# Expert stage of a four-block network: the residual rows of X enter PSUM by identity products, and the output's transposes add onto them

## The reference, cut to what matters

```python
def _L0_ffn_ref(x, Wr, Wg, Wu, Wd, Sg, Su, Sd, expert_bias):
    ...
    rw = jnp.zeros_like(logits).at[jnp.arange(T)[:, None], top_i].set(probs)   # two of eight experts
    gate = jnp.einsum('td,edf->tef', xf, Wg)
    up = jnp.einsum('td,edf->tef', xf, Wu)
    h = jax.nn.silu(gate) * up
    eo = jnp.einsum('tef,efd->ted', h, Wd)
    out = jnp.einsum('te,ted->td', rw, eo)
    out = out + jax.nn.silu(xf @ Sg) * (xf @ Su) @ Sd
...
x = _layernorm(x + _L0_ffn_ref(x, ...), axis=-1)
```

## Time and profile before

| | us |
|---|---|
| median of 3 runs | 2737.09 |
| lowest, highest | 2729.92, 2739.4 |
| span of the profiled execution | 2735.9 |
| of it, the expert stage up to its barrier | about 1192 to 1613 |

### The profile page before, as it was taken

One profiled execution on the slowest core, in us unless ns is written; L12 is line 12 of the kernel. 1 busy time (PEld: TensorE's weight loads), 2 busy tenths in 40 slices (PEclk: granted clock), 3 DMA queues, 4 the chain that ended last, 5 costly groups with the idle time before them and its releaser, 6 DMA issues. The chain is left out here.

```text
span 2735.9 us, 43890 instructions
## 1 busy us (share of the span) xinstructions
PE 2440.4 (89%) x14525; PEld 1454.6 (53%) x14525; DVE 1985.1 (73%) x4362; ACT 1493.0 (55%) x3321; POOL 1309.5 (48%) x1257
## 2 busy tenths in 40 slices
PE   4678989898989898979999979898869999999797
PEld 1224444444444444557777756556644665566555
DVE  4999999999999999536667656777764444455545
ACT  5666777777777775333333324444545556654522
POOL 1777767686767677433333223444563222221411
PEclk7889999999999999999999987999988999999898
DMA  5443444344444444110000143243212000000100
GB/s 161 123 131 121 133 122 128 122 130 122 128 121 127 122 128 132 49 57 18 1 1 1 24 81 65 48 71 69 51 45 60 19 17 17 17 17 17 48 14 9
DMA packets 134306, 195.93 MB, mean 72 GB/s; under 512 B 23953, under 2 KB 58898, under 8 KB 134082
## 3 DMA queue, kind: packets, MB, share of 16 engines
q1 hardware_dynamic: 132098, 190.24, 25.0%
q0 software_dynamic: 960, 2.62, 0.3%
q10 hardware_dynamic: 1024, 0.26, 0.1%
HBM read 153.95 MB, written 13.63 MB: 61 GB/s over the span
## 5 line engine op out<-in xcount | busy, mean ns | idle before, releaser
L398 POOL TENSOR_TENSOR ma_seen<-ma_state,ma_cs 128x1024 f32<-128x1024 f32 x256 | 602.9, 2359 | 324.6 <-DVE ma_state L951 308.4
L951 DVE TENSOR_TENSOR_SCAN ma_state<-ma_decay,ma_last,ma_drive 128x512 f32<-128x512 f32 x512 | 650.8, 1271 | 1.4 <-ACT ma_decay L803 1.3
L587 PE MATMUL ma_acc<-ma_seen,ident 128*128 128x512 f32 x1024 | 493.0, 612 | 45.5 <-POOL ma_seen L398 45.3
L938 DVE TENSOR_TENSOR ma_drive<-ma_weight,ma_bs 128x512 f32<-128x512 f32 x512 | 357.1, 698 | 39.1 <-ACT ma_weight L793 10.6
L587 PEld LDWEIGHTS ma_acc<-ma_seen,ident 128*128 128x128 f32 x1024 | 195.6, 196 | 299.3 <-issue 209.3
L803 ACT ACTIVATE ma_decay<-ma_dt,ma_a_neg 128x512 f32<-128x512 f32 x512 | 338.0, 709 | 0.0
L2076 DVE CUSTOM_DVE_ANT_0 sw_score<-sw_score,both_band 128x256 f32<-128x256 f32 (+1 forms) x512 | 197.6, 449 | 52.5 <-PE sw_score L1890 40.8
L2014 ACT ACTIVATE sw_prob<-sw_turned 128x512 f32<-128x512 f32 (+1 forms) x256 | 135.5, 581 | 180.4 <-PE sw_turned L1904 156.1
L104 POOL TENSOR_TENSOR moe_h_low<-both_V,light_wqkv 128x512 fp32r<-128x512 f32 x80 | 105.0, 1313 | 244.2 <-DVE light_wqkv L100 236.7
L1812 POOL TENSOR_SCALAR_AFFINE_SELECT sw_prob<-sw_prob 128x512 f32<-128x512 f32 x128 | 84.3, 659 | 214.3 <-ACT sw_prob L2014 214.3
L1536 DVE TENSOR_TENSOR both_V<-both_V,moe_up 128x512 f32<-128x512 f32 x80 | 55.0, 688 | 117.3 <-PE moe_up L1325 76.3
(11 more groups left out here) (547 smaller groups left out, 5483.0 us busy)
## 6 DMA issues: line engine op xcount, KB each, us to landing
ma_bs<-bc_rows SPq DMA_DIRECT2D x256, 256.0 KB, 3.3
ma_cs<-bc_rows SPq DMA_DIRECT2D x256, 256.0 KB, 3.3
both_wide<-both_kh SPq DMA_DIRECT2D x28, 192.0 KB, 4.3
both_wide<-both_qh SPq DMA_DIRECT2D x20, 256.0 KB, 4.5
x_rows<-X SPq DMA_DIRECT2D x1, 4096.0 KB
light_rows<-li_y SPq DMA_DIRECT2D x32, 128.0 KB, 1.7
out_dram<-li_o SPq DMA_DIRECT2D x32, 128.0 KB, 1.8
X<-in_L_attn_x_dram SPq DMA_DIRECT2D x1, 3584.0 KB, 14.7
```

Of the source, the lines that this page charges most:

```text
L398: g.tensor_tensor(out=seen[n % RR][:, :, :], in0=state[n % SR][:, :, :], in1=each(cs[n % CR][:, :], 2), op=ALU.mult).then_inc(S["seen_full ...
L587: ins = t.matmul(accs(mm), K["ident"][:, :], seen[n % RR][:, mm, :], start=False, stop=(n % NS == NS - 1))
L938: v.tensor_tensor(out=drive[mm][:, :], in0=weight[mm][:, :], in1=bs[n % CR][:, :], op=ALU.mult).then_inc(S["drive_done"], 1)
L951: v.tensor_tensor_scan(state[n % SR][:, mm, :], decay[s % DR][:, :], drive[mm][:, :], last[:, k, m:m + 1], ALU.mult, ALU.add).then_inc(S[" ...
```

## The change

In each y unit TensorE first multiplies the identity (stationary) with the X rows of the two tiles (256 moving columns each). The first product starts the bank afresh. The four transposes follow in the same bank without the start flag, so that they add onto the X rows; they are written as products with the transpose flag. VectorE copies the bank to y in place of adding X.

```diff
@@ -1299,9 +1299,11 @@
                     pe.wait_ge(S["out_copied0"], i + 1)
                     pe.wait_ge(S["out_copied1"], i + 1)
                     for a in range(2):
+                        t.matmul(to[:, a * D:(a + 1) * D], K["ident"][:, :], X[:, i * GT + 2 * k + a, :], start=(a == 0), stop=False)
+                    for a in range(2):
                         for d in range(DH):
-                            ins = t.transpose(to[:, a * D + d * P:a * D + (d + 1) * P], yT[d][:, (2 * k + a) * P:(2 * k + a + 1) * P],
-                                              K["ident"][:, :])
+                            ins = t.matmul(to[:, a * D + d * P:a * D + (d + 1) * P], yT[d][:, (2 * k + a) * P:(2 * k + a + 1) * P],
+                                           K["ident"][:, :], start=False, stop=(a == 1 and d == DH - 1), is_transpose=True)
                 if kind == "sx":
@@ -1560,8 +1562,7 @@
             def adds(i, b):
                 src = filled("y", i, b)
                 since(dve, "x_done", GT * i)
-                v.tensor_tensor(out=y[:, 2 * b:2 * b + 2, :], in0=src[:, :].rearrange("p (a d) -> p a d", d=D),
-                                in1=X[:, i * GT + 2 * b:i * GT + 2 * b + 2, :], op=ALU.add).then_inc(S["y_done"], 1)
+                v.tensor_copy(y[:, 2 * b:2 * b + 2, :], src[:, :].rearrange("p (a d) -> p a d", d=D)).then_inc(S["y_done"], 1)
```

## The result

The changed kernel takes 2753.87 us (median of 3 runs, 2753.26 to 2761.85) against 2737.09 (2729.92 to 2739.4). The ratio is 1.0066, with a 95% interval of 1.0043 to 1.0090. It is slower by 0.66%, and the profiled span is 2751.8 in place of 2735.9 us, 15.9 us more.

What follows compares the result with a forecast made beforehand. TensorE's own order of work was taken to bound the expert stage; 12.2 us steady plus 2.7 after the loop made 14.9 (13.8 to 16.4), on 2735.9 plus 1.2 for the runs: 2752.0 us, range 2744 to 2759.5.

Steps and rivals of the forecast that it cites:

- What bounds the stage: Expert stage: TensorE's own order of work sets it, busy 300.00 of 300.00 us at clock 1.00.
- Two kinds of extras: Expert slots: eight transposes, or one sv unit's four records, each lengthened a slot by 0.87 us, from about 4.43 to 5.30.
- The price of an identity product: TensorE, expert stage: 0.435 us a product, 0.87 a y unit; slot 5.30 to 7.04 us, 12.2 us over seven groups.
- The form of the transposes: TensorE, y units: transposes with transpose flag and no start flag cost nothing extra; upper bound 7.0 us in all.
- Rival (a): TensorE, y units: each transpose costs two records, 7.0 us more, 2759 us; chance 0.07.
- VectorE: Expert stage: 16 adds of 686 ns become copies of 684 ns from PSUM, gain 0.03 us, taken as none.
- Slack: VectorE's idle time before slot 5's up product stays 1.0 us despite later y units; nothing new waits.
- rival (d): VectorE, expert stage: a new stall if unit 1's copy comes over 1.0 us late, about 2759 us; chance 0.02.
- The tail: Last two y units, after the expert loop: 2.7 us more, between 1.6 at full clock and 4.2 at half.
- rival (b): Next stage's opening: more TensorE work before it holds the clock up, saving 3.0 us, 2747.9 us in all; chance 0.10.
- rival (c): Expert slot 4: another engine sets the pace, products fill waiting; only 2.7 us remain, 2739.8 us; chance 0.05.
- The stages behind "as long as before": Stages after the expert stage: unchanged in length, with the barrier 14 to 16 us later.

Runs made afterwards that it cites:

- the second dose: Changed kernel with every identity product made twice, so X is added twice; 2761.72 us, ratio 1.0092 to the kernel before.
- form_only: Kernel before with only the output transposes rewritten as products with the transpose flag, no identity products, VectorE still adding X; 2732.53 us (one run).
- copy_only: Kernel before with only VectorE's adds replaced by copies, X left out; 2737.67 us (one run).
- warm_products: Kernel before with unread filler products on TensorE around the last y units, two ahead and six behind; 2737.15 us, ratio 1.0026.
- seed_ahead: Changed kernel with the last group's identity products made ahead of TensorE's wait for the output's copies; 2758.71 us, ratio 1.0058.

## Why the prediction was right, point by point

- *What bounds the stage.* Right, and the second dose proves it: 12.1 us for the first, 12.1 for the second. Two kinds of extras that lengthened their slots in full were enough to say so beforehand.
- *The price of an identity product.* 0.87 us a unit forecast, 0.87 measured; slot 7.04 forecast, 7.04 measured; 12.2 us over seven groups forecast, 12.1 measured. Three of the seven y slots grow by 1.72 and not 1.74, from 5.26 to 6.98, which is the missing tenth.
- *The form of the transposes.* Forecast at nothing, and form_only shows nothing. Rival (a) falls.
- *VectorE.* The copy was expected at 684 ns and is 691 in the changed kernel and 686 in copy_only; nothing gained. The second copy was worked out to start 2.84 us after TensorE begins unit 0, and starts 2.81 after. Slack 1.0 forecast, 1.12 seen; rival (d) falls.
- *The tail.* The mechanism was right, and the term was mis-sized in the profiled run: 2.7 us taken, 4.2 measured there, because the clock fell before the y work and not in it. The three traces of the change gave 4.2, 3.1 and 1.6, between the two bounds that stood in the sum. Taking the fall at the place where one trace has it was a choice with no ground: it moves from run to run.
- *The clock giving back,* rival (b). Its mechanism did not occur in the changed kernel: the clock was at half early in the next stage as before, for 6.6 us from the stage's first product on (1632.6 to 1639.2), against 6.2. Its price of 3.0 us stays untested: warm_products gained 1.0 us, but with only 2.8 of the 6.2 us of half clock gone.
- *Not slower,* rival (c). Fell with the slot of 7.04 us.
- *The stages behind "as long as before".* Wrong in this trace. The sliding stage was 3.7 us shorter, while the two half-clock stretches early in the expert stage had cost 3.2. The sum of 14.9 us met the span's 15.9 partly because these two nearly cancel. Neither belongs to the change. The lower heaps lie 12.7 us apart, the profiled parts that belong to it add up to 13.7 to 16.3; I cannot say where that last microsecond or more stays, as the heaps are 7 to 15 us wide in each comparison.
- *The time.* 2752.0 us forecast, 2753.87 measured, and that close a meeting has luck in it. The forecast allowed some 5 us of scatter to each side; it did not know of a second heap some 20 us higher, which held 8 of all 27 runs of the changed kernel. By that share, about one set of three runs in five would have had two or more in it, and a median above the stated range (an estimate from these counts).

## What to carry to other kernels

Where one engine sets the pace, look for a kind of extra work already in the loop and see how much longer its turn is; that gives the price of the next one, to 1% here, while the records' own durations (379 ns for 217 ns of time) do not. Moving an addition onto TensorE as identity products buys nothing when VectorE's instruction stays as long without it, as it does here for a copy out of PSUM. Work that cannot be avoided should at least stand ahead of a wait that does not concern it: in the one trace of seed_ahead that took the whole cost out of the tail, though its times are too scattered to show it.

## What was not expected of the hardware

- An fp32 transpose that adds onto PSUM costs the same as one that does not: eight in 0.87 us, 273 ns a record.
- Transposes alone kept TensorE's clock at 1.00 through 5 us in which it otherwise fell to 0.58 (one trace).
- TensorE can stay at half clock while it is busy 49.78 of 50 us with small products, for 75 us in one trace, and the sliding-window stage then takes 450 to 454 us in place of 427 to 438. This goes with two heaps of times some 20 us apart, in the kernel before, the changed one, seed_ahead and warm_products; a change of 12 us is best read in the parts of a trace that are the same from run to run.
